# Turning token rows and score maxima by transfer instead of by TensorE

## The chip, the cores and the metric

The kernel runs on one core of one Trainium2 chip. The metric is the device time of one launch in microseconds. Three launches of the kernel before took 1077.14, 1079.33 and 1079.54 us; the median is 1079.33 us. A further launch was taken under the hardware profiler, and all rows below are of that one.

## The reference

The kernel computes one pre-norm transformer layer on 32 batches of 256 tokens with 128 features, with 16 heads of 64 features and an inner width of 512. Cut to what matters:

```python
# x: (32, 256, 128)
def attn(query, Wq, Wk, Wv, Wp, bp):
    q = jnp.einsum('bnd,hde->bhne', query, Wq) / sqrt(64)
    k = jnp.einsum('bmd,hde->bhme', query, Wk)
    v = jnp.einsum('bmd,hde->bhme', query, Wv)
    out = jnp.einsum('bhnm,bhme->bnhe', softmax(q k^T), v)
    return jnp.swapaxes(out, -1, -2).reshape(B, N, E * H) @ Wp + bp

def ffn(x, ...):
    h = layer_norm(x, ln1_g, ln1_b)
    h = gelu(h @ ternary(w1).T + b1)
    h = layer_norm(h, ln2_g, ln2_b)
    return h @ ternary(w2).T + b2

x = x + attn(layernorm(x), ...)
x = x + ffn(layernorm(x), ...)
```

## The kernel before, in words

Every float32 factor of a large product is split into a high and a low float16 part, and a product is made of three float16 products (high by high, high by low, low by high). All instructions are placed by hand: each engine has a program of its own, and they meet at semaphores.

The attention runs in steps. A batch has eight steps, j = 0 to 7, one for each pair of heads; the step's number over all batches is t or p. At step t TensorE (PE) runs in this order: `scores(t)` into the one score buffer S; `max_scores(t + 6)`, the high-part scores whose row maxima are taken, into M; `weighted(t - 3)`, the weights times the values, into PV; `queries_keys(t + 8)` into QK; and then what the step's j asks for. That is a quarter of the next batch's values at odd j (`values`), a quarter of the output projection of two batches back at even j (`project`), and the two kinds of transpose that the change is about.

- **The input of a batch, `x`.** GpSimd (POOL) normalises two tiles of 128 tokens into `xn` (line 807) at its step j = 1. At the end of step j = 4 PE transposes both as float32 through the identity matrix into a bank of PSUM (`x_transposed`, line 418). ScalarE (ACT) rounds the result to the high part `xTh` (line 666), and VectorE (DVE) subtracts to get the low part `xTl` (line 947). `queries_keys` reads them four steps later, at j = 0.
- **The shift of the softmax.** DVE writes the negated row maxima of each step into columns of `negmax` (line 962). Every four steps, at the ends of j = 2 and j = 6 (`shift_group`), PE transposes `negmax` as float32 (`shift_turned`, line 515), and DVE copies the result out of PSUM, scaled and rounded to float16, into `shift` (`shift_copied`, line 970, in DVE's next step, behind `qk_low`). `scores` of the steps j = 4 and j = 0 are the first to read it (line 467).

DVE's step t is: `sums_inverse` and `normalise` of the weighted values that PE made in step t - 1 (lines 977, 984), `qk_low` (line 990), then small items, then `max_out(t + 6)` (line 962). PE's next `queries_keys` waits for `qk_low`, its next `weighted` for `normalise`, and its next `max_scores` for `max_out`. ACT's step is the exponentials `p` (line 683), their high part `ph` (line 691), the high part of QK (line 699), and a copy of values or outputs. POOL's step is the low part of the weights, `pl` (line 823), and at some j the norm of the inputs (796 to 815), the low part of the outputs (line 829, j = 0, 2, 4 and 6) and the roots for the feed-forward part (834 to 840).

SyncE (SP) issues all transfers in one queue, in program order. After the loads it only has the DMA transposes of the attention's outputs, `OT<-O`, two for each batch (line 379), at its steps j = 0 and j = 4. Each waits for POOL's low part at that j (`s_olo`), so SP stands at that instruction until POOL is through.

After attention the feed-forward part runs on tiles of 128 tokens, with transposes on PE that the change leaves alone.

Of the kernel before, what the change touches and what calls it, by code (L numbers as in the profile page):

```python
# [72 lines left out]
def x_turn_batch(b, j):  # L73
    return b + 2 if j == 4 and 1 <= b + 2 < B else None
# [48 lines left out]
def misc_uses():  # L123
# [4 lines left out]
    for t in range(-Q_LEAD, NP + TAIL):  # L128
        b, j = divmod(t, HP)
        if shift_group(t) is not None:  # L130
            yield "shift", shift_group(t)
        if x_turn_batch(b, j) is not None:
            yield "x", x_turn_batch(b, j)
# [30 lines left out]
def layer(nc, x_in, wq_in, wk_in, wv_in, wp_in, bp_in, g1_in, lb1_in, w1_in, b1_in,  # L164
          g2_in, lb2_in, w2_in, b2_in, out):
    with ExitStack() as ctx:
# [29 lines left out]
        xTh = [sb(f"xTh{i}", [P, N], F16) for i in range(XT_RING)]  # L196
        xTl = [sb(f"xTl{i}", [P, N], F16) for i in range(XT_RING)]
# [60 lines left out]
        ot_in = [sem(f"s_outputs_transposed{c}") for c in range(H // HH)]  # L258
        stored = sem("s_store")
# [6 lines left out]
        s_xt, s_xhi, s_xlo = sem("s_xT"), sem("s_xT_hi"), sem("s_xT_lo")  # L266
# [6 lines left out]
        s_sht, s_sh16 = sem("s_shift_T"), sem("s_shift_16")  # L273
# [22 lines left out]
        def misc_done(kind, key):  # L296

            return {"x": lambda: (s_xlo, key + 1), "v": lambda: (s_vlo, v_no[key]),
                    "shift": lambda: (s_sh16, key + 1), "y": lambda: (s_x1, key + 1),
# [8 lines left out]
        def head_rows(i):  # L308

            return slice(i * E, (i + 1) * E)  # L310

# [35 lines left out]
        def sp_program(e):  # L347
# [49 lines left out]
        def pe_program(e):  # L397
# [16 lines left out]
            def x_transposed(b):  # L414
                dst = misc_take("x", b)
                e.wait_ge(s_xn, NB * (b + 1))
# [3 lines left out]

            def queries_keys(p):
                b, j = divmod(p, HP)
                r = b % XT_RING
                cols = slice(j * P, (j + 1) * P)
                if j == 0:
                    e.wait_ge(s_xlo, b + 1)
# [6 lines left out]
                for i in range(2):  # L433
                    o = QK[:, i * N:(i + 1) * N]
                    e.matmul(o, Wh[:, i, cols], xTh[r][:, :], start=True, stop=False)  # L435
                    e.matmul(o, Wh[:, i, cols], xTl[r][:, :], start=False, stop=False)  # L436
                    op = e.matmul(o, Wl[:, i, cols], xTh[r][:, :], start=False, stop=True)  # L437
# [62 lines left out]
            def values(b, n):  # L500
                m, half_ = n % 2, n // 2
                r, cols, tok = b % XT_RING, slice(half_ * 512, half_ * 512 + 512), slice(m * P, (m + 1) * P)
                dst = misc_take("v", (b, n))
                if n == 0:
                    e.wait_ge(s_xlo, b + 1)
                if b == 0 and n == 0:
                    e.wait_ge(s_w, W_AT["Wvl"])
                e.matmul(dst[:, :], xTh[r][:, tok], Wvh[:, cols], start=True, stop=False)  # L508
                e.matmul(dst[:, :], xTh[r][:, tok], Wvl[:, cols], start=False, stop=False)  # L509
                e.matmul(dst[:, :], xTl[r][:, tok], Wvh[:, cols], start=False, stop=True).then_inc(s_v, 1)  # L510

            def shift_turned(g):
                dst = misc_take("shift", g)
                e.wait_ge(s_mx, GP * g + GP)
                e.transpose(dst[:, 0:P], negmax[g % 2][:, :], ident[:, :]).then_inc(s_sht, 1)
# [52 lines left out]
            def step(t):  # L568
# [9 lines left out]
                if shift_group(t) is not None:  # L578
                    shift_turned(shift_group(t))
                if x_turn_batch(b, j) is not None:  # L580
                    x_transposed(x_turn_batch(b, j))
# [64 lines left out]
            x_transposed(0)  # L646
# [13 lines left out]
        def act_program(e):  # L660
            def x_high(b):
                e.wait_ge(s_xt, b + 1)
                if b >= XT_RING:
                    e.wait_ge(s_qk, HP * (b - XT_RING) + HP)
                    e.wait_ge(s_v, v_no[b - XT_RING, 3])
                e.activation(xTh[b % XT_RING][:, :], misc("x", b)[:, 0:N], ACT.Copy).then_inc(s_xhi, 1)
# [62 lines left out]
            def step(t):  # L729
# [6 lines left out]
                if x_turn_batch(b, j) is not None:  # L736
                    x_high(x_turn_batch(b, j))
# [38 lines left out]
            x_high(0)  # L776
# [14 lines left out]
        def pool_program(e):  # L791
# [10 lines left out]
            def norm_apply(b):  # L802
                e.wait_ge(s_r0, b + 1)
                if b:
                    e.wait_ge(s_xt, b)
# [96 lines left out]
        def dve_program(e):  # L902
# [40 lines left out]

            def x_low(b):
                e.wait_ge(s_xhi, b + 1)
                r = b % XT_RING
                e.tensor_tensor(xTl[r][:, :], misc("x", b)[:, 0:N], xTh[r][:, :], ALU.subtract).then_inc(s_xlo, 1)
# [9 lines left out]
            def max_out(p):  # L957
                g, jj = divmod(p, GP)
                e.wait_ge(s_ms, 2 * p + 2)
                if jj == 0 and g >= 2:  # L960
                    e.wait_ge(s_sht, g - 1)
                e.tensor_reduce(negmax[g % 2][:, :].rearrange("p (i c) -> p i c", i=2)[:, :, NB * jj:NB * jj + NB],  # L962
# [289 lines left out]
```

## Time and profile before

| | |
|---|---|
| median of 3 launches | 1079.33 us |
| profiled launch | 1075.9 us |
| its span, first to last instruction | 1074.1 us |
| mean granted TensorE clock | 0.988 of full |
| busy PE, ACT, POOL, DVE | 95%, 87%, 83%, 85% of the span |
| DMA engines, 100 us to 940 us | about a quarter of the time |

The span has three stages: a start until about 110 us, in which loads land, weights are prepared and PE often waits; a regular stage until about 940 us; and the feed-forward part. In the regular stage one batch takes 27.2 us. Idle time of an engine counts only where the engine that sets the end waits for it.

### The profile page before, as it was taken

To read this page: it belongs to the slowest core of one execution; us is meant where nothing else is said; L and a number is where in the kernel's file an instruction comes from. 1 tells how busy PE (TensorE), PEld (TensorE's weight loads), DVE (VectorE), ACT (ScalarE), POOL (GpSimd) and SP (SyncE) were. 2 spreads that over 40 slices of the span, in tenths; PEclk is the share of its full clock that TensorE was granted. 3 is DMA by queue.
4 is the path that set the end of the run, shared out by engine and by line. 5 is a ranking of instruction groups with operands and counts; after the bars stand their busy time and mean duration, and the time that the engine had idled before them with its cause. 6 is when DMAs were issued, how large, how long until landed. Compare 5 with 4: busy or idle time off the path is not lost.

```text
span 1074.1 us, 39912 instructions
## 1 busy us (share of the span) xinstructions
PE 1017.7 (95%) x16168; PEld 802.9 (75%) x16168; DVE 908.3 (85%) x1880; ACT 938.8 (87%) x1274; POOL 889.3 (83%) x794
## 2 busy tenths in 40 slices
PE   2878999989899999999999999999999999879998
PEld 1456777767777777777777777778777777668886
DVE  5889888898888888888888888888888888459998
ACT  2677998988799999999999999999999999859996
POOL 3367899998799999999999999999999998944443
PEclk9999999999999999999999999999999999989999
DMA  9202222212222223222222222222222222221111
GB/s 218 52 2 41 42 41 42 38 32 34 41 33 47 39 39 36 42 39 40 41 42 42 41 42 42 41 42 42 42 41 42 41 41 42 42 40 41 31 41 50
DMA packets 159781, 47.51 MB, mean 44 GB/s; under 512 B 141169, under 2 KB 159345, under 8 KB 159601
## 3 DMA queue, kind: packets, MB, share of 16 engines
q1 hardware_dynamic: 159600, 44.97, 23.8%
q8 instruction: 130, 2.13, 0.8%
q14 instruction: 51, 0.41, 0.1%
HBM read 7.21 MB, written 4.19 MB: 11 GB/s over the span
## 4 chain that ended last, share of the span: by engine, by line
PE 83%; DVE 8%; POOL 3%; ACT 3%; issue 3%; DMA 1%; SPq 0%; DVEq 0%; POOLq 0%; ACTq 0%
PE S L475 14%; PE PV L494 7%; PE S L467 7%; PE PV L496 5%; PE PV L495 5%; PE QK L435 5%; PE QK L437 5%; PE QK L436 5%; PE M L448 4%; PE misc L528 2%; PE misc L530 2%; PE misc L529 2%; PE misc L508 2%; PE misc L510 2%; PE misc L509 2%
## 5 line engine op out<-in xcount | busy, mean ns | idle before, releaser
L823 POOL TENSOR_TENSOR pl<-p,ph 128x1024 f16<-128x1024 f32 x256 | 545.8, 2137 | 67.0 <-ACT ph L691 66.9
L683 ACT ACTIVATE p<-S,s_exp 128x1024 f32<-128x1024 f32 x256 | 285.3, 1114 | 55.0 <-PE S L475 52.0
L962 DVE TENSOR_REDUCE negmax<-M 128x4 f32<-128x1024 f32 x256 | 311.9, 1218 | 7.1 <-PE M L448 3.7
L691 ACT ACTIVATE ph<-p 128x1024 f16<-128x1024 f32 x256 | 270.6, 1057 | 8.1
L990 DVE TENSOR_TENSOR QKl<-QK,QKh 128x512 f16<-128x512 f32 x256 | 176.3, 689 | 99.2 <-ACT QKh L699 99.1
L494 PEld LDWEIGHTS PV<-V,ph 128*128 128x128 f16 x2048 | 185.0, 98 | 65.3 <-issue 58.7
L494 PE MATMUL PV<-V,ph 128*128 128x65 f16 x2048 | 215.8, 194 | 11.0 <-DVE O L984 10.7
L495 PE MATMUL PV<-V,ph 128*128 128x64 f16 x2048 | 213.8, 193 | 0.0
L496 PE MATMUL PV<-V,pl 128*128 128x65 f16 x2048 | 213.1, 194 | 0.0
L496 PEld LDWEIGHTS PV<-V,pl 128*128 128x128 f16 x2048 | 188.9, 97 | 0.0
L495 PEld LDWEIGHTS PV<-V,ph 128*128 128x128 f16 x2048 | 188.8, 97 | 0.0
L699 ACT ACTIVATE QKh<-QK 128x512 f16<-128x512 f32 x256 | 148.5, 580 | 24.7 <-PE QK L437 24.7
L435 PE MATMUL QK<-xTh,Wh 128*128 128x256 f16 x512 | 141.2, 276 | 9.8 <-DVE QKl L990 6.5
L829 POOL TENSOR_TENSOR O<-O,O 128x512 f16<-128x512 f32 x128 | 149.3, 1166 | 0.0
L437 PE MATMUL QK<-xTh,Wl 128*128 128x256 f16 x512 | 141.7, 277 | 0.0
L436 PE MATMUL QK<-xTl,Wh 128*128 128x256 f16 x512 | 141.5, 276 | 0.0
L475 PE MATMUL S<-QKh 64*128 64x256 f16 x1024 | 140.4, 271 | 0.0
L475 PE MATMUL S<-QKl,QKh 64*128 64x256 f16 x1024 | 140.3, 270 | 0.0
L475 PE MATMUL S<-QKh,QKl 64*128 64x256 f16 x1024 | 140.2, 270 | 0.0
L984 DVE TENSOR_TENSOR O<-PV,rsum 128x256 f32<-128x256 f32 x256 | 108.7, 425 | 8.8
L467 PE MATMUL S<-shift,sel 64*128 64x256 f16 x1024 | 101.0, 276 | 1.8 <-ACT p L683 1.8
L448 PE MATMUL M<-QKh 64*128 64x256 f16 x1024 | 98.9, 272 | 1.9 <-DVE negmax L962 1.9
(151 smaller groups left out, 2384.3 us busy)
## 6 DMA issues: line engine op xcount, KB each, us to landing
result<-X SPq DMA_DIRECT2D x16, 256.0 KB, 2.3
X<-in_L_attn_query SPq DMA_DIRECT2D x7, 512.0 KB, 7.1
OT<-O SPq DMA_TRANSPOSE x64, 4.5
O<-in_L_attn_Wq SPq DMA_DIRECT2D x1, 512.0 KB, 4.5
O<-in_L_attn_Wk SPq DMA_DIRECT2D x1, 512.0 KB, 6.3
X<-in_L_attn_query SPq DMA_DIRECT2D x2, 256.0 KB, 5.3
O<-in_L_attn_Wv SPq DMA_DIRECT2D x1, 512.0 KB, 5.7
w<-in_L_ffn_w SPq DMA_DIRECT2D x2, 256.0 KB, 5.1
```

The costliest lines, as they stand in the source:

```text
L435: e.matmul(o, Wh[:, i, cols], xTh[r][:, :], start=True, stop=False)
L436: e.matmul(o, Wh[:, i, cols], xTl[r][:, :], start=False, stop=False)
L437: op = e.matmul(o, Wl[:, i, cols], xTh[r][:, :], start=False, stop=True)
L475: op = e.matmul(S[:, i * 512 + m * N:i * 512 + (m + 1) * N], k[rows, 1, tok], q[rows, 0, :], start=False, stop=n == 2, skip_group_check=True)
L494: e.matmul(PV[:, c0:c0 + E + 1], ph[r][:, i, m, tok], v[:, E:2 * E + 1], start=m == 0, stop=False)
L495: e.matmul(PV[:, c0:c0 + E], ph[r][:, i, m, tok], v[:, 0:E], start=False, stop=False)
L496: op = e.matmul(PV[:, c0:c0 + E + 1], pl[r][:, i, m, tok], v[:, E:2 * E + 1], start=False, stop=m == NB - 1)
L683: e.activation(p32[r][:, :, :, :].rearrange("p i m n -> p (i m n)"), S[:, :], ACT.Exp, scale=s_exp[:, :]).then_inc(s_ex, 1)
L691: e.activation(ph[r][:, :, :, :].rearrange("p i m n -> p (i m n)"), p32[r][:, :, :, :].rearrange("p i m n -> p (i m n)"), ACT.Copy).then_i ...
L823: e.tensor_tensor(pl[r][:, :, :, :].rearrange("p i m n -> p (i m n)"), p32[r][:, :, :, :].rearrange("p i m n -> p (i m n)"), ph[r][:, :, : ...
L962: e.tensor_reduce(negmax[g % 2][:, :].rearrange("p (i c) -> p i c", i=2)[:, :, NB * jj:NB * jj + NB], M[:, :].rearrange("p (i t m) -> p i ...
L990: e.tensor_tensor(QKl[p % QK_RING][:, :, :].rearrange("p i n -> p (i n)"), QK[:, :], QKh[p % QK_RING][:, :, :].rearrange("p i n -> p (i n) ...
```

## The change

PE keeps only the first batch's input transposes. For the other 31 batches ACT and DVE split the input in its own layout, tokens on partitions (`xp`, high and low side by side), at j = 3, and SP turns both parts with one DMA transpose of four blocks of 128 by 128 into `xT`. The maxima are rounded in their own layout (`negmax16`), and SP turns them with one DMA transpose of one block straight into `shift`.

```diff
-def x_turn_batch(b, j):
-    return b + 2 if j == 4 and 1 <= b + 2 < B else None
+def x_split_batch(b, j):
+    return b + 2 if j == 3 and 1 <= b + 2 < B else None
...
+        xp = sb("xp", [P, NB, 2, D], F16)
+        xT = [sb(f"xT{i}", [P, NB, 2, P], F16) for i in range(XT_RING)]
...
-        negmax = [sb(f"negmax{i}", [P, P]) for i in range(2)]
+        negmax = [sb(f"negmax{i}", [P, 2, 2 * GP]) for i in range(2)]
+        negmax16 = [sb(f"negmax16_{i}", [P, 2, E], F16) for i in range(2)]
...
+            def turn_x(b):
+                e.wait_ge(s_xlo, b + 1)
+                if b >= XT_RING:
+                    e.wait_ge(s_qk, HP * (b - XT_RING) + HP)
+                    e.wait_ge(s_v, v_no[b - XT_RING, 3])
+                e.dma_start_transpose(xT[b % XT_RING][:, :, :, :].rearrange("p t s n -> p (t s) n"),
+                                      xp[:, :, :, :].rearrange("p t s d -> p (t s d)")).then_inc(xt_in, 16)
+
+            def turn_shift(g):
+                e.wait_ge(s_sh16, g + 1)
+                if g >= 2:
+                    e.wait_ge(s_sc, 2 * GP * (g - 1))
+                e.dma_start_transpose(shift[g % 2][:, :].unsqueeze(1),
+                                      negmax16[g % 2][:, :, :].rearrange("p i c -> p (i c)")).then_inc(shift_in, 16)
...
                 if t is not None:
+                    if shift_group(t) is not None:
+                        turn_shift(shift_group(t))
+                    if x_split_batch(*divmod(t - 1, HP)) is not None:
+                        turn_x(x_split_batch(*divmod(t - 1, HP)))
                     for b, c in turned_halves(*divmod(t, HP)):
                         turn_outputs(b, c)
...
                 if jj == 0:
-                    e.wait_ge(s_sh16, g + 1)
+                    e.wait_ge(shift_in, 16 * (g + 1))
...
-                if shift_group(t) is not None:
-                    shift_turned(shift_group(t))
-                if x_turn_batch(b, j) is not None:
-                    x_transposed(x_turn_batch(b, j))
...
             def x_high(b):
-                e.wait_ge(s_xt, b + 1)
...
+                e.wait_ge(s_xn, NB * (b + 1))
+                if b >= 2:
+                    e.wait_ge(xt_in, 16 * (b - 1))
+                e.activation(xp[:, :, 0, :], xn[:, :, :], ACT.Copy).then_inc(s_xhi, 1)
...
             def x_low(b):
                 e.wait_ge(s_xhi, b + 1)
...
+                e.tensor_tensor(xp[:, :, 1, :], xn[:, :, :], xp[:, :, 0, :], ALU.subtract).then_inc(s_xlo, 1)
...
-            def shift_copied(g):
-                e.wait_ge(s_sht, g + 1)
+            def shift_rounded(g):
+                e.wait_ge(s_mx, GP * g + GP)
                 if g >= 2:
-                    e.wait_ge(s_sc, 2 * GP * (g - 1))
-                e.tensor_scalar(shift[g % 2][:, :], misc("shift", g)[:, 0:P], 1.0 / SHIFT_UP, None,
+                    e.wait_ge(shift_in, 16 * (g - 1))
+                e.tensor_scalar(negmax16[g % 2][:, :, 0:2 * GP], negmax[g % 2][:, :, :], 1.0 / SHIFT_UP, None,
                                 ALU.mult).then_inc(s_sh16, 1)
...
                         normalise(before - PV_LAG)
+                    if shift_group(t) is not None:
+                        shift_rounded(shift_group(t))
                     if 0 <= before + Q_LEAD < NP:
                         qk_low(before + Q_LEAD)
-                    if shift_group(before) is not None:
-                        shift_copied(shift_group(before))
```

Of SP's queue this is one stretch of the kernel before in the regular stage; the `OT` rows are the two halves of the outputs of one batch, then of the next.

```order
L379 DMA_TRANSPOSE OT0_1<-O16_1 128x16x128 [waits s_y,s_o_lo]
L379 DMA_TRANSPOSE OT1_0<-O16_0 128x16x128 [waits s_y,s_o_lo]
L379 DMA_TRANSPOSE OT1_1<-O16_1 128x16x128 [waits s_y,s_o_lo]
L379 DMA_TRANSPOSE OT0_0<-O16_0 128x16x128 [waits s_y,s_o_lo]
L379 DMA_TRANSPOSE OT0_1<-O16_1 128x16x128 [waits s_y,s_o_lo]
```

The same place after the change:

```order
L388 DMA_TRANSPOSE xT2<-xp 128x4x128 [waits s_v,s_qk,s_x_lo]
L380 DMA_TRANSPOSE OT0_1<-O16_1 128x16x128 [waits s_y,s_o_lo]
L395 DMA_TRANSPOSE shift0<-negmax16_0 128x1x128 [waits s_scores,s_shift_16]
L380 DMA_TRANSPOSE OT1_0<-O16_0 128x16x128 [waits s_y,s_o_lo]
L395 DMA_TRANSPOSE shift1<-negmax16_1 128x1x128 [waits s_scores,s_shift_16]
L388 DMA_TRANSPOSE xT0<-xp 128x4x128 [waits s_v,s_qk,s_x_lo]
```

Each shift now stands right behind an output half in the one queue, and the input of a batch stands ahead of the second half.

On DVE, from `QKl` (the low part of queries and keys) of step j = 2 to step j = 4 of one batch, in the kernel before:

```order
L990 TENSOR_TENSOR QKl5<-QK,QKh5 128x512
L996 TENSOR_TENSOR V1<-misc1,V1 128x8x64
L962 TENSOR_REDUCE negmax0<-M 128x2x2
L977 RECIPROCAL rsum1<-PV 128x4
L984 TENSOR_TENSOR O1<-PV,rsum1 128x2x128
L990 TENSOR_TENSOR QKl6<-QK,QKh6 128x512
L970 TENSOR_SCALAR shift1<-misc1 128x128
L962 TENSOR_REDUCE negmax0<-M 128x2x2
L977 RECIPROCAL rsum0<-PV 128x4
L984 TENSOR_TENSOR O0<-PV,rsum0 128x2x128
L990 TENSOR_TENSOR QKl7<-QK,QKh7 128x512
L996 TENSOR_TENSOR V1<-misc1,V1 128x8x64
```

The same stretch after it, with the rounding that stands just ahead of that `QKl`:

```order
L995 TENSOR_SCALAR negmax16_1<-negmax1 128x2x8
L1015 TENSOR_TENSOR QKl5<-QK,QKh5 128x512
L1021 TENSOR_TENSOR V1<-misc1,V1 128x8x64
L987 TENSOR_REDUCE negmax0<-M 128x2x2
L1002 RECIPROCAL rsum1<-PV 128x4
L1009 TENSOR_TENSOR O1<-PV,rsum1 128x2x128
L1015 TENSOR_TENSOR QKl6<-QK,QKh6 128x512
L987 TENSOR_REDUCE negmax0<-M 128x2x2
L1002 RECIPROCAL rsum0<-PV 128x4
L1009 TENSOR_TENSOR O0<-PV,rsum0 128x2x128
L1015 TENSOR_TENSOR QKl7<-QK,QKh7 128x512
L972 TENSOR_TENSOR xp<-xn,xp 128x2x128
```

The rounding of the maxima has moved one step earlier and ahead of `QKl`, and it reads SBUF where the copy read PSUM. The low part of the input, which stood in step j = 5, has moved to j = 4, ahead of the values' low part, and has both of its inputs in SBUF.

On PE, the end of a step j = 2 before, where the misc1 row is the transpose of the maxima:

```order
L435 MATMUL QK<-xTh2,Wh 128x256
L436 MATMUL QK<-xTl2,Wh 128x256
L437 MATMUL QK<-xTh2,Wl 128x256
L515 MATMUL misc1<-ident,negmax0 128x128
L528 MATMUL misc0<-Wph,OT0_1 128x128
L529 MATMUL misc0<-Wpl,OT0_1 128x128
```

And after:

```order
L461 MATMUL QK<-xT2,Wh 128x256
L462 MATMUL QK<-xT2,Wh 128x256
L463 MATMUL QK<-xT2,Wl 128x256
L549 MATMUL misc0<-Wph,OT0_1 128x128
L550 MATMUL misc0<-Wpl,OT0_1 128x128
L551 MATMUL misc0<-Wph,OT0_1 128x128
```

Nothing takes the transpose's place there; step j = 4 loses its two input transposes in the same way.

## Rows read from the trace of the kernel before

**Rows 1.** The page: busy time by engine, and the chain that ended last.

```profile
PE 1017.7 (95%) x16168; PEld 802.9 (75%) x16168; DVE 908.3 (85%) x1880; ACT 938.8 (87%) x1274; POOL 889.3 (83%) x794
...
PE 83%; DVE 8%; POOL 3%; ACT 3%; issue 3%; DMA 1%; SPq 0%; DVEq 0%; POOLq 0%; ACTq 0%
```

**Rows 2.** Windows, one batch: us, PE, PEld, DVE, ACT, POOL busy; PEclk, DMA share, GB/s.

```profile
500.87:528.07 27.20, 27.20 (x466) 21.62 (x468) 23.44 (x50) 25.56 (x34) 25.89 (x21) 1.00 0.25 41
```

**Rows 3.** Waits, 400 to 900 us: total, times, longest.

```profile
ACT p L683 <- PE S L475: 23.9, 129, 0.3
POOL pl L823 <- ACT ph L691: 15.4, 39, 1.2
```

**Rows 4.** The chain of waits, 500 to 530 us, pieces on PE: start, length.

```profile
500.87 0.32 PE S L467 x4
...
507.56 0.32 PE S L467 x4
...
510.25 0.11 PE misc L515
...
511.03 0.33 PE S L467 x4
...
514.36 0.33 PE S L467 x4
...
517.05 0.22 PE misc L418 x2
...
517.94 0.33 PE S L467 x4
...
528.07 0.32 PE S L467 x4
```

**Rows 5.** Groups by line on DVE: busy us, mean ns.

```profile
L970 DVE TENSOR_SCALAR shift<-misc 128x128 f16<-128x128 f32 x64 | 18.0, 281 | 0.0
L947 DVE TENSOR_TENSOR xTl<-misc,xTh 128x256 f16<-128x256 f32 x32 | 13.3, 415 | 0.0
```

**Rows 6.** Tile OT from 100 to 940 us, and SP's timeline: start, length.

```profile
L379 SPq DMA_TRANSPOSE OT<-O x61: 1687/1927/3157, 114.0 to 938.7; - x61
...
DMA to landing us min/median/max: 4.2/4.6/6.0
...
509.10 1.91 SPq L379 DMA_TRANSPOSE OT<-O  x1
...
522.08 2.94 SPq L379 DMA_TRANSPOSE OT<-O  x1
```

**Rows 7.** The page, DMA issues: KB each, median us to landing.

```profile
result<-X SPq DMA_DIRECT2D x16, 256.0 KB, 2.3
```

**Rows 8.** Timeline of POOL, 500 to 529 us: start, length.

```profile
500.92 2.13 POOL L823 TENSOR_TENSOR pl<-p,ph 128x1024 f16<-128x1024 f32 x1 [0.22 <-ACT ph L691]
...
507.92 1.16 POOL L829 TENSOR_TENSOR O<-O,O 128x512 f16<-128x512 f32 x1
...
513.51 2.13 POOL L823 TENSOR_TENSOR pl<-p,ph 128x1024 f16<-128x1024 f32 x1
...
520.91 1.15 POOL L829 TENSOR_TENSOR O<-O,O 128x512 f16<-128x512 f32 x1
```

**Rows 9.** Timeline of DVE, the start of its step j = 2.

```profile
506.84 0.42 DVE L984 TENSOR_TENSOR O<-PV,rsum 128x256 f32<-128x256 f32 x1
507.99 0.69 DVE L990 TENSOR_TENSOR QKl<-QK,QKh 128x512 f16<-128x512 f32 x1 [0.73 <-ACT QKh L699]
```

**Rows 10.** Timelines of DVE and POOL near 79 us, then near 99 us.

```profile
79.33 1.93 DVE L1035 TENSOR_SCALAR clip<-sums 128x2 f32<-128x2 f32 x1
...
79.11 2.12 POOL L823 TENSOR_TENSOR pl<-p,ph 128x1024 f16<-128x1024 f32 x1
...
99.02 2.63 DVE L1047 TENSOR_TENSOR tern<-above,below 128x512 f32<-128x512 f32 x1
...
101.05 1.61 POOL L829 TENSOR_TENSOR O<-O,O 128x512 f16<-128x512 f32 x1
```

More of the change, by code:

```diff
@@ L298, in misc_done @@
             return {"x": lambda: (s_xlo, key + 1), "v": lambda: (s_vlo, v_no[key]),
-                    "shift": lambda: (s_sh16, key + 1), "y": lambda: (s_x1, key + 1),
+                    "y": lambda: (s_x1, key + 1),
                     "turn": lambda: (s_w, W_AT[f"top_{key}"]), "spread": lambda: (s_w, W_AT[f"clip_{key}"]),
@@ L310, in head_rows, with xT_part @@
             return slice(i * E, (i + 1) * E)
+        def xT_part(b, part_):
+            return xT[b % XT_RING][:, :, part_, :]
         def pv_parts():
@@ L419, in x_transposed, with wait_x @@
                 op.then_inc(s_xt, 1)
+            def wait_x(b):
+                if b == 0:
+                    e.wait_ge(s_xlo, 1)
+                else:
+                    e.wait_ge(xt_in, 16 * b)
             def queries_keys(p):
                 b, j = divmod(p, HP)
-                r = b % XT_RING
+                xh, xl = xT_part(b, 0), xT_part(b, 1)
                 cols = slice(j * P, (j + 1) * P)
                 if j == 0:
-                    e.wait_ge(s_xlo, b + 1)
+                    wait_x(b)
                 if p == 0:
@@ L433, in queries_keys @@
                 for i in range(2):
[L434 to L437, printed above, removed]
+                    o = QK[:, i * N:(i + 1) * N].rearrange("p (t n) -> p t n", t=NB)
+                    e.matmul(o, Wh[:, i, cols], xh, start=True, stop=False)
+                    e.matmul(o, Wh[:, i, cols], xl, start=False, stop=False)
+                    op = e.matmul(o, Wl[:, i, cols], xh, start=False, stop=True)
                 op.then_inc(s_qk, 1)
@@ L501, in values @@
                 m, half_ = n % 2, n // 2
-                r, cols, tok = b % XT_RING, slice(half_ * 512, half_ * 512 + 512), slice(m * P, (m + 1) * P)
+                xh, xl, cols = xT_part(b, 0)[:, m, :], xT_part(b, 1)[:, m, :], slice(half_ * 512, half_ * 512 + 512)
                 dst = misc_take("v", (b, n))
                 if n == 0:
-                    e.wait_ge(s_xlo, b + 1)
+                    wait_x(b)
                 if b == 0 and n == 0:
                     e.wait_ge(s_w, W_AT["Wvl"])
[L508 to L515, printed above, removed]
+                e.matmul(dst[:, :], xh, Wvh[:, cols], start=True, stop=False)
+                e.matmul(dst[:, :], xh, Wvl[:, cols], start=False, stop=False)
+                e.matmul(dst[:, :], xl, Wvh[:, cols], start=False, stop=True).then_inc(s_v, 1)
             def project(b, t, c):
@@ L660, in act_program, with first_x_high @@
         def act_program(e):
+            def first_x_high():
+                e.wait_ge(s_xt, 1)
+                e.activation(xT_part(0, 0), misc("x", 0)[:, 0:N].rearrange("p (t n) -> p t n", t=NB),
+                             ACT.Copy).then_inc(s_xhi, 1)
             def x_high(b):
-                e.wait_ge(s_xt, b + 1)
[L663 to L666, printed above, removed]
+                e.wait_ge(s_xn, NB * (b + 1))
+                if b >= 2:
+                    e.wait_ge(xt_in, 16 * (b - 1))
+                e.activation(xp[:, :, 0, :], xn[:, :, :], ACT.Copy).then_inc(s_xhi, 1)
             def w_high(j):
@@ L735, in step @@
                     qk_high(t + Q_LEAD)
-                if x_turn_batch(b, j) is not None:
-                    x_high(x_turn_batch(b, j))
+                if x_split_batch(b, j) is not None:
+                    x_high(x_split_batch(b, j))
                 if first_values(t) is not None:
@@ L942, in norm_stats, with first_x_low @@
                     e.bn_aggr(mv0[:, t, :], st0[:, t, :]).then_inc(s_mv, 1)
+            def first_x_low():
+                e.wait_ge(s_xhi, 1)
+                e.tensor_tensor(xT_part(0, 1), misc("x", 0)[:, 0:N].rearrange("p (t n) -> p t n", t=NB), xT_part(0, 0),
+                                ALU.subtract).then_inc(s_xlo, 1)
             def x_low(b):
                 e.wait_ge(s_xhi, b + 1)
-                r = b % XT_RING
-                e.tensor_tensor(xTl[r][:, :], misc("x", b)[:, 0:N], xTh[r][:, :], ALU.subtract).then_inc(s_xlo, 1)
+                e.tensor_tensor(xp[:, :, 1, :], xn[:, :, :], xp[:, :, 0, :], ALU.subtract).then_inc(s_xlo, 1)
             def w_low(j):
@@ L1194, in dve_program @@
             w_low(0)
-            x_low(0)
+            first_x_low()
             w_low(1)
```

33 lines of the change are left out of this document (14 added, 19 removed).

## The prediction

> **What bounds the kernel now.** I read the page's busy shares and chain first: PE is busy 95% of the span and holds 83% of the chain that ended last [rows 1]. Then the windows, because an average hides stages: in one batch of the regular stage PE is busy all 27.20 us at full clock, POOL 25.89, ACT 25.56 and DVE 23.44 [rows 2]. The waits of that stage say how near the next engine is: in the 500 us from 400 to 900, which is 18.4 batches, ACT waits 23.9 us for PE and POOL 15.4 us for ACT [rows 3], or 1.3 and 0.84 us a batch. So left to themselves ACT would need about 25.9 us a batch and POOL 26.4. PE sets the pace, and POOL stands 3% behind it.
>
> **What is removed.** The chain of waits gives the starts of `scores` step by step, and so what a transpose costs PE in place, where its own duration overlaps its neighbours'. The step from 507.56 to 511.03, with the transpose of maxima in it, takes 3.47 us; the next, from 511.03 to 514.36, has none and takes 3.33; the one with the two input transposes, 514.36 to 517.94, takes 3.58 [rows 4]. The chain itself holds 0.11 and 0.22 us of them; the rest is what stands around a float32 operation between float16 ones. So a shift transpose is worth 0.14 us, an input pair 0.25, and a batch 0.14 + 0.14 + 0.25 = 0.53 us: 27.20 goes to 26.67. They count only where PE is the bound. In the start, until about 110 us, PE waits for weights and for DVE; I leave out 7 of the 64 shifts and 3 of the 31 pairs and get 57 x 0.14 + 28 x 0.25 = 15.0 us as the ceiling. DVE also loses 64 copies of 281 ns out of PSUM [rows 5], which lie in the shadow of PE in the regular stage and are worth nothing there.
>
> **What is added on ACT.** The high part of the input has the same 256 elements, from SBUF in place of PSUM, and moves into j = 3. ACT waits 1.3 us a batch and comes down to 0.8 when PE gains 0.53, so it has room for some tenths; exponentials of step j = 4 begin perhaps 0.2 us late and are done over half a microsecond before PE needs the score buffer. Nothing.
>
> **What is added in SP's queue.** This is the term that decides. A shift now travels DVE, SP, DMA, and PE's `scores` of j = 4 and j = 0 wait for its landing. SP is in order, and ahead of the shift of j = 2 stands an output half that waits for POOL's low part. In the trace that low part begins at 507.92 and lasts 1.16 us [rows 8], and the output transpose is issued at 509.10 for 1.91 us, so the shift can't be issued before 511.01 although its data are rounded by about 508. The deadline is `scores` of j = 4 at 514.36, or 514.22 with one transpose less ahead of it: 3.2 us from issue to landing. For the other shift the output half is issued at 522.08 for 2.94 us [rows 6], SP is free at 525.02, and the deadline is 528.07 - 0.53 = 527.54 [rows 4]: 2.5 us. No row shows a transpose of one block. Upper bound: one of 16 blocks lands in 4.2 to 6.0 us, median 4.6, with 1.7 to 3.2 us of that on SP [rows 6]. Lower bound: a sixteenth of the shortest, 0.3 us. The nearest row in size is the store of 256 KB, whose landing takes 2.3 us [rows 7]; the shift moves 32 KB. I take 2 us, which meets both deadlines by 0.5 to 1.2 us.
>
> But the shift's packets queue on the same DMA engines behind those of the output half. The DMA share of a quarter over 27.2 us [rows 2] is 3.4 us for each of the two output halves, so a one-block transpose adds about 0.2 us of its own, and I let the shift land 0.3 us behind the half. Then 509.10 + L + 0.3 has to be under 514.22: L under 4.8 us. The median landing, 4.6, makes it; the longest, 6.0, misses by 1.2 [rows 6]. If a third of the halves are over 4.8, by 0.6 on average, that is 0.2 us at this deadline. At the other, 522.08 + L + 0.3 under 527.54 wants L under 5.2, so somewhat less is lost, and a stall at one deadline gives room at the next. I take 0.2 us a batch in all, 31 x 0.2 = 6 us.
>
> The Trainium skill (page "VectorE: DVE Perf Modes", section "The three transpose paths") gives 1309 ns for one 128 by 128 transpose by the DMA crossbar against 390 ns on TensorE, and advises TensorE where a PSUM destination will do. Its 1309 ns would put a shift issued at 511.01 at 512.3, ahead of the deadline. That advice speaks against the change; here the destination had to be copied out of PSUM as well, and PE is the bound, so I don't follow it. No run here shows the figure.
>
> The input's transfer has four steps from landing to use and is issued while SP is idle. It costs at most 4/16 of an output half on the DMA engines, which are idle three quarters of the time [rows 2]: nothing.
>
> **What is added on DVE, and against POOL.** The rounding is 16 elements, the low part of the input 256. But they no longer read PSUM, and the trace shows what that does while POOL is at work: a scalar operation on 2 elements began at 79.33 and took 1.93 us, to the end of the `pl` that POOL had begun at 79.11; and POOL's 512-element low part after a DVE operation with two SBUF inputs took 1.61 us at 101.05, against 1.16 elsewhere [rows 10, 8]. So each engine waits for the end of the other's instruction. `xTl` and the shift copy from PSUM did not: their means are 415 and 281 ns [rows 5].
>
> The Trainium skill (page "SBUF — State Buffer", section "Who interferes with whom") states it as a lock of a shared port pair, taken by a DVE instruction with two SBUF inputs or by a scalar operation in a two-port mode, and held for a whole instruction. The trace agrees: 1.93 us for two elements.
>
> Each of the three new DVE operations of a batch can so wait from nothing to one `pl`, 2.13 us. In j = 2, DVE has 0.73 us of idle time between `normalise` and `QKl` [rows 9], in which the rounding stands, and POOL is then in short work of the norm ahead of the 507.92 operation [rows 8], so the wait is about 0.7 us and covered. In j = 6 POOL ends a `pl` about when the rounding comes (its next operation begins at 520.91 [rows 8]); covered too. The low part of the input comes at about 515.4 and waits for the `pl` that began at 513.51 [rows 8], some 0.2 us. Behind it stand the values' low part and `max_out`, then `normalise`, which PE's `weighted` needs 1.1 us after `scores` of j = 5; the reserve is a few tenths. I take 0.05 us a batch from all three, 1.5 us. POOL itself pays for the low part of the input, some 0.25 us: 26.4 becomes 26.6, just under PE's 26.67. That cover is thin, and with another 0.3 us POOL is the bound (below).
>
> **The sum.** Against the profiled launch, 1075.9 us (span 1074.1 and 1.8 around it): 1075.9 - 15.0 + 6 + 1.5 = 1068.4. That launch is 3.4 us under the median of the three, 1079.33. The same 7.5 us off the median gives **1071.8 us**. Bounds from the unknown costs: with neither stalls nor locks 1064.3; with the shift at the landing of a whole output half, 1094 (below).
>
> **The rivals.**
> 1. *The full gain.* Landing of the halves doesn't hold the shift, because its packets overlap theirs. For it: the first deadline leaves 3.2 us, against 2.3 for a larger store. Against: one queue, landings up to 6.0. Time: 1079.3 - 15 = 1064.3.
> 2. *The shift lands late every time*, as long after its issue as the shortest output half, 4.2 us. For it: no row shows that blocks, not a fixed part, make those 4.2 us. Against: 3.4 us of DMA work in each. The loop is: from POOL's `pl` of j = 7 at 500.92 to the issue of the half 8.18 us, SP 1.91, landing 4.2, so `scores` of j = 4 stands 14.29 us behind that `pl`; from there to the next such `pl` it is 528.12 - 514.36 - 0.39 = 13.37. Sum 27.66, 0.46 over the present 27.20, times 31: 1079.3 + 14 = 1093.6. It decides from a landing of 3.7 us, where the loop equals 27.20.
> 3. *The locks reach PE.* POOL is at work 95% of the time, so phases may fall badly: if two of the three waits last 0.4 us more than DVE's reserve, 0.8 - 0.53 = 0.27 us a batch are lost, 1087.7. It decides from 0.27 us each. Against: the phases above.
> 4. *POOL becomes the bound* at 26.4 + 0.3 to 0.7 for locks taken in turn, so 26.7 to 27.1: the gain shrinks to 3 us or so, 1076 us. For it: POOL's 0.84 us of waiting is all it has. Such a delay of POOL also delays the output half and with it the shift.
>
> **Chances.** The forecast with part of the gain, 1066 to 1076 us, has 0.37; full gain 0.24; the late shift 0.17; locks 0.12; POOL 0.10. A measurement of this kernel can tell about 0.3%, 3.2 us, from no change. Faster by more than that: most of the first, all of the second and a fifth of the last, 0.61. Within it: 0.13. Slower: 0.26. The forecast's own range is 1066 to 1076; the one for 8 in 10 runs from 1062.5, under the ceiling by the spread of the launches, to 1090, which takes in the locks and cuts the late shift.
>
> **What would show it.** A batch in the regular stage of 26.8 to 26.95 us; steps without the 0.14 and 0.25 us; PE waits at `scores` for the DMA of `shift` in some batches only, under 1 us each, where the output half lands 5 us or more after issue; landing of a shift around 2 us from its issue; the rounding lasting up to 2 us at times, with no PE wait behind it; POOL's waits for ACT down to 0.3 us a batch. The prediction is wrong if PE waits for `shift` in every batch, if the batch is 27.2 us or longer, or if PE waits for `QKl` or `O`.

## The result, and the profile after

The changed kernel takes 1086.3 us (median of 4, 1084.8 to 1088.1), the kernel before in its four launches 1078.2 (1076.5 to 1079.5): a ratio of 1.0077, 95% interval 1.0050 to 1.0103. The forecast was 1071.8 us and faster; it became slower, above the forecast's own range (1066 to 1076 us) and inside the wide one (up to 1090). The profiled launch of the changed kernel took 1088.1 us with a span of 1086.3, that of the kernel before 1075.9 with 1074.1, so 12.2 us have to be found between the two spans.

The page of the changed kernel, busy time by engine, the chain that ended last, the group of `scores`' first matmuls, and the DMA issues with the median us to landing:

```profile
PE 1008.2 (93%) x16042; PEld 789.5 (73%) x16042; DVE 934.0 (86%) x1880; ACT 937.9 (86%) x1274; POOL 893.6 (82%) x794
...
POOL 34%; PE 32%; issue 9%; DVE 8%; DMA 7%; ACT 6%; SPq 4%; POOLq 0%; DVEq 0%; ACTq 0%
...
L493 PE MATMUL S<-shift,sel 64*128 64x256 f16 x1024 | 100.9, 276 | 20.1 <-DMA shift<-negmax 19.1
...
shift<-negmax SPq DMA_TRANSPOSE x64, 2.8
...
OT<-O SPq DMA_TRANSPOSE x64, 4.4
```

PE did 9.5 us less work than in [rows 1], but its share of the chain fell from 83% to 32%, and POOL, DMA and SP's queue came in with 45%. PE waited 19.1 us for the shift. The waits from 400 to 900 us (total, times, longest) answer to [rows 3]:

```profile
ACT p L704 <- PE S L501: 28.4, 126, 1.3
PEld S L493 <- DMA shift<-negmax: 22.6, 27, 1.9
...
POOL pl L844 <- ACT ph L712: 11.3, 11, 1.2
PE S L493 <- DMA shift<-negmax: 9.7, 13, 1.4
```

There are 36 shifts in that stretch, and the weight load in front of `scores` waits for 27 of them. The chain of waits of the changed kernel, 585 to 605 us (start, length), shows a whole round. It answers to [rows 4]:

```profile
585.78 2.14 POOL pl L844
587.92 1.12 POOL O L850
589.05 0.09 issue
589.14 2.13 POOL pl L844
...
592.92 2.13 POOL pl L844
...
596.12 1.17 POOL O L850
597.31 1.79 SPq L380
599.20 4.41 DMA shift<-negmax
603.65 0.39 PE S L493 x4
```

POOL works back to back from the `pl` of j = 6, which begins 3.39 us after PE's `scores` of that step (582.39), to the low part of the first output half, at j = 0 of the next batch. SP issues that half for 1.79 us, and only then the shift of j = 2, which lands 4.41 us after its own issue. `scores` of j = 4 begin at 603.65; those of the batch before, in the same chain, at 575.63. What doesn't depend on the landing is 6.76 from there to `scores` of j = 6, 3.39 to the `pl`, 11.53 on POOL and 1.89 on SP, together 23.6. So the loop is 23.6 us + L, where L is the time from the issue of the shift to its landing. It exceeds PE's own batch, 26.77 (experiment 1), from L = 3.2 us.

A batch is measured here from one start of POOL's operation `mr` to the next, which comes once a batch. The text ahead of the prediction lets the start end at 110 us. In fact six batches more, until 314 us before and 319 us after the change, have the feed-forward weights prepared beside them, and only the 21 after them, to 885 and 895 us, are regular:

| kernel | batch, mean (lowest to highest) | six batches with weights, 136 to 320 us |
|---|---|---|
| before | 27.21 (27.20 to 27.21) | 177.1 |
| changed | 27.40 (26.76 to 28.27) | 183.5 |

So the 12.2 us are: 21 x 0.19 = 4.1 in the regular stage; 6.4 in the batches with weights; 3.3 in the last batch (28.02 in place of 24.51, less 0.2 in the one before); and -1.6 at the start and the end. The last batch is one wait: its steps have less work for PE, the shift issued at 927.08 landed 4.5 us after the issue, and PE waited 4.29 us for it.

### The profile page after: what moved, and what is told of

It is laid out like the page before. It is cut to its first block, busy times and chain, and to the rows that moved or that the text cites. A ratio compares the mean times of both kernels' runs of the same rounds, so it can differ in the third digit from the quotient of the medians.

```text
span 1086.3 us, 39752 instructions
## 1 busy us (share of the span) xinstructions
PE 1008.2 (93%) x16042; PEld 789.5 (73%) x16042; DVE 934.0 (86%) x1880; ACT 937.9 (86%) x1274; POOL 893.6 (82%) x794
## 4 chain that ended last, share of the span: by engine, by line
POOL 34%; PE 32%; issue 9%; DVE 8%; DMA 7%; ACT 6%; SPq 4%; POOLq 0%; DVEq 0%; ACTq 0%
POOL pl L844 20%; POOL O L850 7%; DMA shift<-negmax 6%; PE S L501 5%; SPq L380 3%; ACT p L704 3%; PE S L493 2%; PE PV L520 2%; ACT ph L712 2%; DVE negmax L987 2%; POOL r L857 2%; PE QK L461 1%; POOL xn L828 1%; PE QK L463 1%; PE QK L462 1%
## 5 line engine op out<-in xcount | busy, mean ns | idle before, releaser
L520 PE MATMUL PV<-V,ph 128*128 128x65 f16 x2048 | 216.7, 194 | 12.0 <-DVE O L1009 11.9
L850 POOL TENSOR_TENSOR O<-O,O 128x512 f16<-128x512 f32 x128 | 152.6, 1192 | 0.0
L461 PE MATMUL QK<-xT,Wh 128*128 128x256 f16 x512 | 141.9, 277 | 10.5 <-DVE QKl L1015 7.3
L463 PE MATMUL QK<-xT,Wl 128*128 128x256 f16 x512 | 142.5, 278 | 0.0
L462 PE MATMUL QK<-xT,Wh 128*128 128x256 f16 x512 | 142.3, 278 | 0.0
L493 PE MATMUL S<-shift,sel 64*128 64x256 f16 x1024 | 100.9, 276 | 20.1 <-DMA shift<-negmax 19.1
```

What stands on the lines that cost most here:

```text
L462: e.matmul(o, Wh[:, i, cols], xl, start=False, stop=False)
L463: op = e.matmul(o, Wl[:, i, cols], xh, start=False, stop=True)
L520: e.matmul(PV[:, c0:c0 + E + 1], ph[r][:, i, m, tok], v[:, E:2 * E + 1], start=m == 0, stop=False)
L850: e.tensor_tensor(o16(k, 1), o_rows(b, k), o16(k, 0), ALU.subtract).then_inc(s_olo, 1)
```

## The experiments

Each group ran on one chip beside 15 to 17 launches of the kernel before.

**1. SP's order.** Both output halves are issued behind the shift:

```diff
 def turned_halves(b, j):
-    last = 4 if b < B else 3
-    return [(b - back, c) for c, (at, back) in enumerate(((0, 1), (last, 1))) ...
+    first, last = (2, 6) if b < B else (0, 3)
+    return [(b - back, c) for c, (at, back) in enumerate(((first, 1), (last, 1))) ...
```

> The changed kernel with one thing moved: in SP's queue both output halves of a batch are issued behind the shift of maxima of their neighbourhood in place of ahead of it. Queue theory (the shift stands behind an output half, lands about 3.6 us after the half's end of issue, holds PE at the scores of j = 4 and closes a loop through POOL of 27.2 us or more): the wait of PE for the shift goes, the batch falls from 27.39 to about 26.7 us, and the time is 1062 to 1070 us, faster than the kernel before. Lock theory (DVE's three new operations in SBUF and POOL wait for each other, and that delay reaches PE): nothing of it is changed, the time stays at 1083 us or more.

Measured: 1069.07 us, ratio 0.9922 (0.9904 to 0.9940). The batch is 26.77 us, each one between 26.76 and 26.77, and no wait for `shift` is left. The tile `shift` from 400 to 900 us, first of the changed kernel and then of this one (count, ns on SP, lowest, median and highest; landing in us):

```profile
L395 SPq DMA_TRANSPOSE shift<-negmax x36: 1183/1608/1853, 407.6 to 886.4; - x36
...
DMA to landing us min/median/max: 2.3/2.9/4.7
```

```profile
L395 SPq DMA_TRANSPOSE shift<-negmax x38: 1120/1122/2159, 399.4 to 894.8; - x38
...
DMA to landing us min/median/max: 2.2/2.3/4.2
```

SP's timeline of this kernel near 508 us (start, length):

```profile
506.47 1.12 SPq L395 DMA_TRANSPOSE shift<-negmax  x1
508.20 2.02 SPq L380 DMA_TRANSPOSE OT<-O  x1
```

One block takes 2.2 us to land in most cases when nothing stands just ahead of it, but up to 4.2. The shift now goes out 1.73 us before the half, where it went 1.89 us behind the half's start (597.31 to 599.20 above). That is 3.6 us earlier, enough for the late landings too. The order is worth 17 us. The queue theory holds and the lock theory, which had 1083 or more, falls.

**2. Only the first half moved**, `(2, 1), (4, 1)` in place of `(2, 1), (6, 1)`:

> The changed kernel with only the first output half moved behind the shift of j = 2 in SP's queue; the second half still stands ahead of the shift of j = 6. Queue theory with the loop through j = 4 alone: this half is the one that matters, the batch is 26.77 us as in e3_order and the time within 3 us of it, 1067 to 1072. Rival (each half ahead of its shift costs its share, as the prediction had it with two deadlines, the second with only 2.5 us): half of the loss stays, 1076 us or more.

Measured: 1075.09 us, ratio 0.9980 (0.9967 to 0.9993), mean batch 27.11 (26.76 to 27.91). I had taken the loop through j = 4 for the only one; that was wrong. Its waits from 400 to 900 us:

```profile
PEld S L493 <- DMA shift<-negmax: 8.8, 10, 1.3
...
PE S L493 <- DMA shift<-negmax: 3.9, 7, 0.8
```

All ten waits are at the other deadline, `scores` of j = 0. The last batch is back at 24.52. So of the 17 us, moving the half ahead of the shift of j = 2 gives back 11, and moving the other 6 more.

**3. One more block ahead of each shift**, which nothing reads:

```diff
             def turn_shift(g):
+                ...
+                e.dma_start_transpose(idle_block[:, :].unsqueeze(1), sel[:, 0, :]).then_inc(idle_in, 16)
                 e.wait_ge(s_sh16, g + 1)
```

> The changed kernel with one more transpose of one block issued by SP just ahead of every shift, into a buffer that nothing reads. DVE, ACT, POOL and PE do exactly the same work. Queue theory: every shift is issued 1.2 us later, the loop through POOL and the landing grows by 1.2 us and is now the longest in every batch: 28.3 to 28.9 us, a time of 1110 to 1128 us. Lock theory: the time stays within 3 us of the changed kernel. A rival of the queue theory (the shift has room for another microsecond and only rare late landings hurt): under 1097 us.

Measured: 1115.33 us, ratio 1.0359 (1.0335 to 1.0383), batch 28.47. The waits from 400 to 900 us:

```profile
PEld S L500 <- DMA shift<-negmax: 41.9, 31, 2.8
...
PE S L500 <- DMA shift<-negmax: 26.9, 24, 2.3
```

The time is in the range expected, but the delay was not the 1.2 us that I had set down. Between the end of the half's issue and the issue of the shift lie 1.8 us on average in place of 0.1 (400 to 880 us). Part of it came back, because the shift then landed sooner after its own issue: counted from the end of the half's issue the landing moved by 0.9 us for the shifts of j = 2 (3.6 to 4.5) and by 1.6 for those of j = 6 (3.0 to 4.5). The batch grew by 1.07 us, near the first delay and far below the sum of both, 2.5. That is what a loop through one landing does; two stalls that simply add would have given the sum.

**4. The two halves of the change alone.** `shift_only` leaves the input on PE, `x_only` the maxima, each with the code of the kernel before for the other.

> The other half: maxima rounded in their layout and turned by a transfer, the input transposed on PE as before. Queue theory: the loop through the shift is as in the changed kernel and sets the batch, so PE's 0.25 us for the input stand in its shadow: 1084 to 1089 us, as slow as the whole change. Lock theory: two short meetings with POOL are left of three: 1080 to 1083 us.

> Half of the change: the input is split and turned by a transfer, the maxima are transposed on PE as before. Queue theory: no transfer is left whose landing PE waits for soon, so the 0.25 us a batch of the input pair come in, 28 x 0.25 = 7 us less about 1 for one DVE operation that can meet POOL: about 1072 us. Lock theory: one of the three meetings a batch is left (the 256-element one is the longest), so half of the loss stays and the time is 1079 us or above.

Measured: `shift_only` 1084.85, ratio 1.0074 (1.0056 to 1.0092), batch 27.56, as the queue theory had it: this part alone is as slow as the whole change. `x_only` 1075.84, ratio 0.9995 (0.9984 to 1.0006): no gain and no loss, which neither theory had. Yet every batch of its regular stage takes 26.98 to 27.00 us. 21 x 0.22 = 4.6 us came in there and 6.7 were lost in the batches with weights, 183.8 in place of 177.1 us. This loss the changed kernel has too (183.5), and the queue has no part in it: in `x_only` PE waits for no transfer in these batches. In `shift_only` they take 178.4 us.

Where it lies is seen on DVE. The kernel before near 235 us, and then `x_only` (start, length, line):

```profile
234.00 1.22 DVE L962 TENSOR_REDUCE negmax<-M 128x4 f32<-128x1024 f32 x1
235.13 4.63 DVE L1064 TENSOR_SCALAR above<-tern,gs 128x128 f32<-128x128 f32 x4
...
239.89 0.42 DVE L984 TENSOR_TENSOR O<-PV,rsum 128x256 f32<-128x256 f32 x1
```

```profile
233.31 1.08 DVE L971 TENSOR_TENSOR xp<-xn,xp 128x256 f16<-128x256 f32 x1
234.31 0.68 DVE L1020 TENSOR_TENSOR V<-misc,V 128x512 f16<-128x512 f32 x1
234.91 1.21 DVE L986 TENSOR_REDUCE negmax<-M 128x4 f32<-128x1024 f32 x1
236.04 5.70 DVE L1088 TENSOR_SCALAR above<-tern,gs 128x128 f32<-128x128 f32 x4
...
241.87 0.42 DVE L1008 TENSOR_TENSOR O<-PV,rsum 128x256 f32<-128x256 f32 x1
```

A burst of four scalings of the feed-forward weights stands in step t = 52, the j = 4 of a batch. The low part of the input was made one step later before the change, and now in the same step ahead of the burst. `O` comes 1.98 us later, and PE, which had already waited for it, waits longer. Its first `weighted` matmul with the idle time before it, in the kernel before and in `x_only`:

```profile
240.46 0.19 PE L494 MATMUL PV<-V,ph 128*128 128x65 f16 x1 [2.96 <-DVE O L984]
```

```profile
242.44 0.22 PE L512 MATMUL PV<-V,ph 128*128 128x65 f16 x1 [5.22 <-DVE O L1008]
```

Then the granted clock falls, which it had not done here in the profiled launch of the kernel before. Windows of the kernel before, of `x_only` and of `shift_order` (experiment 7, with the input on PE) (us, busy time of PE, PEld, DVE, ACT and POOL with their counts, PEclk, DMA share, GB/s):

```profile
240.00:244.00 4.00, 3.54 (x60) 2.65 (x61) 3.97 (x8) 1.50 (x3) 1.83 (x1) 1.00 1.12 129
244.00:248.00 4.00, 4.00 (x87) 3.52 (x84) 3.35 (x8) 3.71 (x5) 1.96 (x1) 1.00 0.04 9
```

```profile
240.00:244.00 4.00, 1.56 (x26) 1.52 (x27) 3.96 (x6) 0.00 (x0) 1.66 (x1) 0.58 0.70 131
244.00:248.00 4.00, 4.00 (x29) 2.09 (x27) 1.94 (x5) 1.19 (x2) 0.00 (x0) 0.57 0.03 6
```

```profile
240.00:244.00 4.00, 3.67 (x33) 2.51 (x33) 3.09 (x8) 0.60 (x1) 1.71 (x1) 0.50 0.02 4
```

From 244 to 248 us PE is busy all the time in the first two, but 0.57 is a mixture of the two levels, for the most part 1.2 GHz. (The counts, 29 matmuls and 87, are not the price: in `x_only` they are the wider ones.) The batch that holds the burst lasts 35.95 us in place of 31.59, 4.4 us more. The longer wait is 2.3 of them. The other 2.1 go with the clock, and they can't be put down to the input's part alone: in `shift_order` PE waits 2.94 us here, as long as in the kernel before, the clock falls all the same, and the batch lasts 34.20 us.

A second place is a meeting of DVE and POOL. DVE and then POOL of `x_only`, at 176 us:

```profile
176.49 2.32 DVE L971 TENSOR_TENSOR xp<-xn,xp 128x256 f16<-128x256 f32 x1
```

```profile
176.40 4.40 POOL L843 TENSOR_TENSOR pl<-p,ph 128x1024 f16<-128x1024 f32 x2
```

The low part waits out the first of POOL's two `pl`, and takes 2.32 us where it takes 0.50 to 0.52 in the 18 batches from 400 to 900 us. Here DVE has a bias row of the weights beside it and no reserve: PE waits 1.34 us for the maxima behind it, and that batch is 1.5 us longer than before. No run took the meeting away, so that it is the cause is argued from these waits.

**5. The meetings in the regular stage.** Order of experiment 1, with the rounding on ACT:

```diff
-                e.tensor_scalar(negmax16[g % 2][:, :, 0:2 * GP], negmax[g % 2][:, :, :], 1.0 / SHIFT_UP, None,
-                                ALU.mult).then_inc(s_sh16, 1)
+                e.activation(negmax16[g % 2][:, :, 0:2 * GP], negmax[g % 2][:, :, :], ACT.Copy,
+                             scale=1.0 / SHIFT_UP).then_inc(s_sh16, 1)
```

> The order of e3_order in SP's queue, and the rounding of the maxima (16 elements) moved from DVE to ACT, ahead of the step's exponentials, so that it can't meet POOL. Queue theory: within 2 us of e3_order. Lock theory: the two meetings a batch at the rounding are gone, so it is faster than e3_order by 3 us or more.

Measured: 1069.94 us, ratio 0.9931 (0.9912 to 0.9950), batch 26.77. In this order the waits of the rounding for POOL cost nothing.

**6. The crowded step.** In `x_only` the burst is moved as it is, and the bias row:

```diff
-GAINS1, LESS_LAST, BIAS1, BIAS1_ROW = 18, 24, 32, 35
-T1_SPLIT, GAINS2, MEAN2, T2_SPLIT, BIAS2 = MAXIMA["t1"][2] + 1, 52, 56, 58, 64
+GAINS1, LESS_LAST, BIAS1, BIAS1_ROW = 18, 24, 32, 37
+T1_SPLIT, GAINS2, MEAN2, T2_SPLIT, BIAS2 = MAXIMA["t1"][2] + 1, 53, 56, 58, 64
```

> x_only with two numbers changed: the burst of four scalings of the second matrix goes as it is from step 52 to 53, and the addition of a bias row from step 35 to 37, so that neither shares a step with the low part of the input. Theory of the crowded step (x_only gained 0.22 us in each of some 27 batches and lost 6.7 us in the stretch of the weights, 4.3 at the burst and 1.5 at the bias row): 1068 to 1071 us, and the six intervals of that stretch take 177 us or less, as in the kernel before, in place of 183.8. Rival (the input's operations cost this stretch their time wherever the weights' operations stand): 1074 us or more.

Measured: 1072.65 us, ratio 0.9960 (0.9946 to 0.9974), six batches 180.7. That is between the two. By the starts of `scores`, the four steps with the burst fell from 21.1 us to 17.5 (16.7 before the change), so the burst's neighbour was the cause there, of the wait (now 2.33 us) and with it of a part of the lower clock. The three steps at the bias row rose from 11.9 to 12.5: that guess was wrong. The low part still took 2.31 us, and the bias row itself now 2.15 in place of 1.33.

**7. The shift alone, in the better order.**

> shift_only with the order of e3_order in SP's queue: the maxima alone are turned by a transfer, each ahead of the output half, and the input stays on PE. Queue theory: no wait for the shift, batch 27.20 - 0.22 = 26.98 us, the stretch of the weights loses 1.4 us as in shift_only: 1069 to 1071 us, so that the input's part adds nothing to e3_order as it stands. Rival (the shift's transfers cost something of their own on the DMA engines or at POOL's port even in this order): 1074 us or more.

Measured: 1070.11 us, ratio 0.9939 (0.9917 to 0.9961), batch 26.99. As expected. Beside experiment 1, at 0.9922 (0.9904 to 0.9940), the input's part of the change adds nothing that can be told from the noise: what it gains in the regular stage (21 x 0.22 us) it gives back in the batches with weights (183.0 us in experiment 1, 178.7 here).

**8. The burst spread out**, on experiment 1 and on the kernel before. One of the four operations in each of four steps, and the same for another burst, four replications of a bias at step 64. `e3_spread` also moves the bias row from step 35 to 37, as in experiment 6; `b_spread` leaves it:

```diff
-T1_SPLIT, GAINS2, MEAN2, T2_SPLIT, BIAS2 = MAXIMA["t1"][2] + 1, 52, 56, 58, 64
+T1_SPLIT, GAINS2, MEAN2, T2_SPLIT, BIAS2 = MAXIMA["t1"][2] + 1, (47, 51, 53, 55), 56, 58, 64
...
-                if t == GAINS2:
-                    for c in range(FC):
-                        op = e.tensor_scalar(above[1][:, c * D:(c + 1) * D], ...
-                    weight(op, "T2")
+                if t in GAINS2:
+                    c = GAINS2.index(t)
+                    op = e.tensor_scalar(above[1][:, c * D:(c + 1) * D], ...
+                    if c == FC - 1:
+                        weight(op, "T2")
```

> e3_order, and in the stretch where the feed-forward weights are prepared: the four scalings of the second matrix, which all stand in one step (t = 52, the step in which the low part of the input is now made), go one each into steps 47, 51, 53 and 55; the four replications of the second bias from step 64 into 57, 61, 62 and 63; and the addition of a bias row from step 35 to 37, away from the low part of another batch. Theory of the crowded step (the low part of the input pushes DVE's burst 1.1 us and more back, PE waits 5.2 us in place of 3.0, and the granted clock falls to about 0.6 for some 7 us, 4.3 us in all; 1.6 us more at the bias row): that batch falls from 34.9 to about 29 us, and the time is 1057 to 1063 us. Rival (the stretch loses its time to the transfers of the input or to meetings with POOL wherever the operations stand): 1066 us or more.

> The kernel before with the same spreading of the two groups of four operations (its bias row stays). It says how much of e3_spread comes from a stall that the kernel before had already. Theory of the crowded step: the 3.0 us of waiting at each of the two groups go, partly given back as short waits: 1071 to 1073 us, a gain of 3 to 5 us, so about half of what e3_spread gains over e3_order. Rival (the stretch's loss has nothing to do with the burst): both kernels gain the same or nothing.

Measured: `e3_spread` 1058.32 us, ratio 0.9820 (0.9798 to 0.9843), faster than both kernels; `b_spread` 1068.73, ratio 0.9924 (0.9907 to 0.9942), more than the 3 to 5 us I had given it. The six batches took 171.8 and 169.6 us. 135 to 320 us, experiment 1 and then `e3_spread`:

```profile
135.00:320.00 185.00, 172.83 (x2831) 134.80 (x2830) 170.18 (x316) 157.64 (x204) 159.49 (x130) 0.97 0.26 43
```

```profile
135.00:320.00 185.00, 179.22 (x3029) 140.70 (x3027) 172.35 (x333) 167.07 (x217) 170.03 (x137) 1.00 0.26 47
```

The clock is whole, and 3029 matmuls fit where 2831 did. The spreading gives 10.8 us to experiment 1 and 7.1 to the kernel before: two waits of 3.0 us were there already, the second with a fall of the clock behind it, and the change had made the two bursts 3.7 us dearer. (The bias row has no visible share in that: its batch takes 30.6 us in `e3_spread` and 30.2 in experiment 1.)

## Why the prediction was wrong, step by step

- **PE's gain.** The mechanism was right, the size a fifth too large. The kernel before needs 27.21 us, `x_only` 26.99, `shift_order` 26.99, both together 26.77: 0.22 for an input pair, 0.11 for a shift, 0.44 a batch, and not 0.53. These are the transposes' own lengths in the chain of [rows 4]. The extra "what stands around a float32 operation" is not there. I had compared a step with a transpose to its neighbour, and the two kinds differ without one. In the chain of experiment 1 (start, length) the step that ends with the values (L534) takes 3.33 us, and the next, with the projection, 3.36:

```profile
423.03 0.33 PE S L493 x4
425.71 0.22 PE misc L534
...
426.36 0.32 PE S L493 x4
...
429.72 0.33 PE S L493 x4
```

- **The step that failed: the landing of the shift**, taken as 2 us, or 0.3 us behind the half, and so late in a third of the cases only, 0.2 us a batch. Alone in the queue a block mostly does land after 2.2 us. Behind a half it took 2.3 to 4.7 us from its own issue: it landed mostly 0.2 to 1.0 us after the half, at times 1.1 to 2.4. And SP held it for 1.6 us in place of 1.1. Against the order of experiment 1 this cost 0.63 us a batch, three times what was set down, and 3.5 us once in the last batch, which the prediction had not looked at: there PE's steps are short and every deadline is earlier.
- **How often it is late.** The slack of 3.2 us was right. Of the 18 shifts for j = 4 from 400 to 880 us, 11 are over it, by 0.8 us on average and up to 4.4 from the issue (median of both kinds 2.9, in the rows of experiment 1): 0.5 us a batch at this deadline alone. Nine of the 11 stand behind a half that landed 5.1 to 6.2 us after its issue. The prediction let a third of the halves be over 4.8; in the trace of the kernel before, 26 of the 61 halves of [rows 6] are.
- **A stall at one deadline as room for the next.** I had let the two stalls partly cancel. Experiment 3 says instead that late landings close a loop through POOL, in which each microsecond over the slack lengthens the batch. Rival 2 had the loop, 23.46 us + L; the chain gives 23.6 + L. It also had its point of decision, 3.7 us against the old batch. Against the faster batch of 26.77, which the forecast itself counted on, it is 3.2. The batch of 27.66 that rival 2 gave for L = 4.2 is near what such batches show (27.5 to 28.3); its price, every time, was too high, and the true mean was 27.40.
- **The DMA share.** One block adds little work, as said. It is the place in one queue that costs. The Trainium skill (page "DMA: Bandwidth & Descriptors", section "Queues, rings and completion order") has the increment of a transfer's semaphore land only after all earlier writes of that DMA engine. The trace agrees with it: no shift lands before the half ahead of it, and behind a half that took 5.8 us or more it took 3.9 us or more itself, mostly 0.2 us after the half.
- **Locks**, 0.05 us a batch. They exist: the rounding took 0.16 to 1.18 us from 400 to 900 us. In the regular stage they cost nothing (experiment 5, and `x_only` at 26.99). Rival 3 falls. One meeting outside that stage goes with 1.5 us.
- **The input's part: nothing on ACT and in the queue, and on DVE its share of the 0.05 us.** Right in the regular stage, wrong outside it, and the second term that was missing. I read the regular stage only, and costed the move of the low part from one step to the one before where DVE has room. In the batches with weights it has none: they take 6.4 us more in the changed kernel and 6.7 in `x_only`, of which 3.1 are back once the burst stands one step later. With the input on PE they take about 1.5 us more (`shift_only`, `shift_order`), after a wait no longer than before and a fall of the clock, so one profile of each can't split the sum to the microsecond.
- **POOL as the bound** (rival 4): not seen. In `e3_order` POOL still waits 3.4 us from 400 to 900 us, and the batch is PE's.
- The Trainium skill's advice (page "VectorE: DVE Perf Modes", section "Rules for kernel authors") to leave such a transpose on TensorE stood against the change. The 1309 ns in the same page's section "The three transpose paths" compare with 1.12 us on SP and 2.2 to the landing here. In the order of the change the advice held. With the shift ahead of the half it did not: 1070.11 us with the maxima turned by a transfer (experiment 7) against 1076.07 with TensorE.

What stays open: why some transposes land 1 to 2 us later than others of the same size. With nothing just ahead of them there are such landings too: in `shift_order` 12 of the 38 shifts from 400 to 900 us landed over 3.2 us after their issue, up to 4.1, and nothing waited for them. An estimate from these: the same landings at a slack of 3.2 us would cost 0.17 us a batch, against 0.5 behind the half. So a part of the lateness is not the half's doing, and no run here separates the two.

## What to carry to other kernels

A transfer that the bottleneck engine waits for must not stand behind a larger one in its queue, nor behind a wait of the issuing engine for something slow; here both came together, and no run weighs them apart. Order a queue by deadline, and look at the loop that it closes: once the landing is over the slack, each microsecond is lost once a batch. A move by one step that is free in the regular stage has to be read again in every stage that isn't regular: where weights are prepared beside the work, and in the last batch. And if an engine is already waited for in one step, a burst there is the first thing to spread.

## What the runs showed of the hardware

- The same wait of TensorE can leave the granted clock whole or let it fall. At the first burst, near 237 us, it stayed at 2.4 GHz through an idle time of 2.96 us in the kernel before, but fell with 2.94 us in `shift_order` (0.50 from 240 to 244 us, in the rows of experiment 4) and with 2.33 us in `x_moved` (0.74 in the same window). After 5.22 us in `x_only` PE ran for the most part at 1.2 GHz for some 5 us. At the other burst, near 281 us, a wait of 3.03 us was followed by a fall in the kernel before too. With both bursts spread out the clock stayed whole from 135 to 320 us. Two windows of the kernel before:

```profile
280.00:286.00 6.00, 2.97 (x25) 2.58 (x25) 4.92 (x12) 1.86 (x3) 5.42 (x8) 0.81 0.00 0
286.00:292.00 6.00, 6.00 (x101) 4.51 (x101) 3.75 (x7) 4.19 (x5) 2.03 (x1) 0.91 0.48 90
```

- A DMA transpose of one block of 128 by 128 in float16 mostly lands 2.2 us after its issue, with 1.1 us on SP, but up to 4.2 us after it with nothing just ahead; one of four blocks mostly after 2.4 us; one of 16 after 4.2 to 6.5.
- A subtraction on DVE with two SBUF inputs and 256 elements took 2.32 us beside a `pl` of POOL that began 0.09 us before it, and 0.50 to 0.52 in a phase without such a meeting.
